# Graph attention layer, last stage: the large piece of scores and flags comes as two pieces, issued behind the landing of the chains' additions

## Chip, cores and metric

One core of one Trainium2 chip runs the whole kernel. The metric is the device time of one execution in microseconds, the median of several runs.

## What is computed

The reference is one layer of a graph network with 6,250 nodes, 200,000 edges (sorted by destination) and 8 heads, with a residual and a layer norm behind it. Cut to what matters here:

```python
qk = jnp.sum(q[:, dst] * rel_k, -1) / 4.0                 # a score for each edge and head
m = segment_max(qk.T, dst); se = segment_sum(exp(qk.T - m[dst]), dst)
lse = log(se) + m                                         # a log-sum for each node and head
logw = qk - lse.T[:, dst]
agg = segment_sum(logw[..., None] * rel_v, dst)           # sums over the edges of a node
z = layer_norm(relu(agg @ z_W + z_b), z_g, z_beta)
x = layer_norm(x + z)
```

As the weights are qk minus lse, the sums over edges fall apart: one sum of qk times rel_v, and one of rel_v alone that is later multiplied by lse. So the edge stage can store sums before any lse is known.

## The kernel before

The first two stages (`start` and `edges`, about 2750 us) compute tables of the nodes and run over the edges in groups of 512. They leave three things in DRAM: `edge_qk`, the scores by head; `edge_fresh`, flags in bf16 that say where a new destination begins; and `tile_sums`, the sums over each tile of 128 edges by destination. A destination whose edges run over several tiles has its sum in parts; the *chains* add these parts along the tiles with a scan, and the results are added onto rows of `tile_sums`.

The last stage (`tail`) has three strands.

- **Log-sums.** 128 partitions (16 chunks of the edges times 8 heads) hold 12,544 scores each in `t_x` and as many flags in `t_fresh`, in 14 sub-pieces of `SUB` = 896 columns (`NSUB` = 14). For each sub-piece k, DVE scans a running maximum (line 1791), computes ratios (1796, 1797, into a ring of `RS` = 4 buffers) and scans the running sum of the sub-piece before (1781). PE subtracts the maximum (2168, 2169), ACT takes the exponential (2016, 2018) and, two sub-pieces later, the logarithm (1998). PE then turns the log-sums of sub-piece k - 3 (2153, 2154), ACT copies them into one of `LR` = 2 buffers `t_lse_sb` (`copy_lse`, 2008 and 2009), and SP stores that buffer, 448 KB, into `edge_lse` (line 1746). `copy_lse(k)` for k of 2 and more waits until store k - 2 has landed. DVE's ratio of sub-piece k waits for PE's turn of sub-piece k - 4.
- **Sums.** POOL first issues 13 indirect DMAs that add the chains' results onto `tile_sums` (line 1694, semaphore `s_add`), waits until all have landed (line 1697), and then gathers the sums of 36 blocks of 128 nodes (line 1703). Then it waits for all stores of log-sums and gathers these by node (line 1711), 49 gathers, with the 13 gathers of sums that are left between them.
- **Turns.** 13 turns of up to four blocks of nodes combine sums and log-sums, multiply with z_W, norm and store; DVE's first row of a turn that needs gathered log-sums is line 1893.

**How scores and flags arrive.** `PARTS` names the pieces in sub-pieces: 0, 1, 2 to 3, 4 to 7, 8 to 13. The first three are loaded in the edge stage. Piece 3 (scores 1792 KB, flags 896 KB) and piece 4 (scores 2688 KB, flags 1344 KB) are loaded in `tail`: the scores by SP, one behind the other, when the chains' last transpose is done (`s_cb` at 7, since the chains use the same columns of `t_x`); the flags by ACT (`load_fresh`), piece 3 early, piece 4 at its sub-piece 1. DVE waits for a piece's semaphore `s_x`, scores and flags, at the piece's first sub-piece. SP's instructions run in order: behind the two issues of scores come the 14 stores of log-sums, then loads of x.

DMAs of SP, of ACT and of POOL go into three queues: in the views q1 is that of SP, q10 that of ACT, q0 that of POOL.

Of the kernel before, what the change touches and what calls it, by code (L numbers as in the profile page):

```python
# [12 lines left out]
KT = -(-E // (P * P))  # L13
# [31 lines left out]
FIRSTS_AT = 385  # L45
NSUB = 14
SUB = CE // NSUB
PARTS = [(0, 1), (1, 2), (2, 4), (4, 8), (8, NSUB)]
HALF = KT * P
CHAIN_AT = GROUPS + 3  # L50
ROWS_AT = GROUPS + 7
# [80 lines left out]
def chain_views(t):  # L132

    x = t["x"]
    st = x[:, PARTS[3][0] * SUB:PARTS[3][0] * SUB + 2 * HALF]
    at = PARTS[3][0] * SUB + 2 * HALF + 32
    return x[:, at:at + 2 * HALF], st, x[:, at + 2 * HALF:at + 3 * HALF]
# [37 lines left out]
class Phase:  # L175
# [8 lines left out]
    def sem(self, name):  # L184
        self.sems.append(self.nc.alloc_semaphore(name=name))
        return self.sems[-1]
# [823 lines left out]
def edges(nc, a, t):  # L1010
# [79 lines left out]
    def is_group(x, loop):  # L1090
# [4 lines left out]
                                                      "chain_back", "chain_back_copied")}  # L1095
    passed.update({f"x_piece{i}": nc.alloc_semaphore(name=f"x_piece{i}") for i in range(len(PARTS))})
    s_fl, s_fm, s_fh, s_more = (passed[n] for n in ("firsts_low", "firsts_mid", "firsts_high", "chains_loaded"))
    s_ct, s_cc, s_cs, s_cb, s_cbc = (passed[n] for n in ("chain_T", "chain_T_copied", "chain_summed", "chain_back", "chain_back_copied"))
    s_x = [passed[f"x_piece{i}"] for i in range(len(PARTS))]

# [12 lines left out]
    with nc.Block(no_gpsimd_drain=True) as block:  # L1113
        @block.sync
        def _(sp):
# [12 lines left out]
            def load_piece(k):  # L1128

                a0, a1 = PARTS[k]  # L1130
                b = -(-((CHUNKS - 1) * CE + a1 * SUB) // BE) - 1
# [444 lines left out]
def tail(nc, a, t, out):  # L1576
# [63 lines left out]
    s_fh, s_ct, s_cc, s_cs, s_cb, s_cbc = (passed[n] for n in ("firsts_high", "chain_T", "chain_T_copied", "chain_summed", "chain_back", "chain_back_copied"))  # L1640
    s_x = [passed[f"x_piece{i}"] for i in range(len(PARTS))]
    s_pre, s_ch, s_add = sem("tail_pads"), sem("tail_dve_chain"), sem("chain_added")
# [16 lines left out]
    def turn(n):  # L1659

        if not 0 <= n < TURNS:
            return None
        whole = n < TURNS - 1 or BLOCKS % NBK == 0 and LAST == P
        return (NBK, P) if whole else (BLOCKS - NBK * n, LAST)
# [18 lines left out]
    with nc.allow_non_contiguous_dma(reason="rows of 512 bytes"), nc.Block(no_gpsimd_drain=True) as block:  # L1683
# [43 lines left out]
        @block.sync  # L1727
        def _(sp):
            rows = t["qk_d"].rearrange("h (c e) -> (h c) e", e=CE)
            sp.wait_ge(s_pre, 1)  # L1730
            sp.dma_start(t["qk_d"][:, E:PLACES], low).then_inc(s_low, 16)
            for k in (3, 4):
                a0, a1_ = PARTS[k]
                sp.wait_ge(s_cb, 7)
                if k == 4:
                    sp.wait_ge(s_low, 16)
                sp.dma_start(x[:, a0 * SUB:a1_ * SUB], rows[:, a0 * SUB:a1_ * SUB]).then_inc(s_x[k], 16)
            def load(n):
                if turn(n):
                    nb, rows = turn(n)  # L1740
                    sp.dma_start(xb[n % XBR][0:rows, 0:nb, :],
                                 a["x"][P * NBK * n:P * NBK * n + nb * rows, :].rearrange("(b p) f -> p b f", p=rows)).then_inc(s_xl[n % XBR], 16)

            for k in range(NSUB):
                sp.wait_ge(s_lc, 2 * (k + 1))
                sp.dma_start(t["lse_d"].rearrange("(e c) h -> e (c h)", c=CHUNKS)[k * SUB:(k + 1) * SUB, :].rearrange("(t p) c -> p t c", p=P), lse_sb[:, k % LR, :, :]).then_inc(s_ls[k % LR], 16)
            sp.wait_ge(s_d, NSUB)
            for n in range(XBR):
                load(n)
            for q in range(LR):  # L1750
                sp.wait_ge(s_ls[q], 16 * len(range(q, NSUB, LR)))
            for n in range(TURNS):
                nb, rows = turn(n)
                sp.wait_ge(s["o"], n + 1)
                sp.dma_start(out[P * NBK * n:P * NBK * n + nb * rows, :].rearrange("(b p) f -> p b f", p=rows), o[n % 2][0:rows, 0:nb, :]).then_inc(s_o[n % 2], 16)
                load(n + XBR)
            for q in range(2):
                sp.wait_ge(s_o[q], 16 * len(range(q, TURNS, 2)))

        @block.vector  # L1760
        def _(dve):
# [22 lines left out]
            for k in range(NSUB):  # L1784
                lo, hi = k * SUB, (k + 1) * SUB
                for part, (a0, _) in enumerate(PARTS):
                    if k == a0:
                        dve.wait_ge(s_x[part], 32)
                if k >= 1:
                    dve.wait_ge(s_m, k)  # L1790
                v.tensor_tensor_scan(out=m[:, lo + 1:hi + 1], data0=fresh[:, lo:hi], data1=x[:, lo:hi],
                                     initial=m[:, lo:lo + 1] if k else -BIG, op0=ALU.add, op1=ALU.max).then_inc(s_m, 1)
                dve.wait_ge(s_m, k + 1)
                if k >= RS:
                    dve.wait_ge(s_t, k - RS + 1)
                link(v.tensor_tensor(out=ratio[:, k % RS, :], in0=m[:, lo:hi], in1=m[:, lo + 1:hi + 1], op=ALU.subtract))
                v.tensor_tensor(out=ratio[:, k % RS, :], in0=ratio[:, k % RS, :], in1=fresh[:, lo:hi], op=ALU.add).then_inc(s_d, 1)
                if k == 0:
                    dve.wait_ge(s_cc, 7)
                    dve.wait_ge(s_cs, 4)  # L1800
                    for half in range(2):
                        chain_scan(v, t, 2, half).then_inc(s_cs, 1)
                if k >= 1:
                    run_sum(k - 1)
# [167 lines left out]
        def _(act):  # L1972
            flags = t["fresh_d"].rearrange("(c e) -> c e", e=CE)

            def load_fresh(k):
                a0, a1_ = PARTS[k]
                act.dma_start(fresh[:, a0 * SUB:a1_ * SUB], flags[:, a0 * SUB:a1_ * SUB].unsqueeze(0).to_broadcast([H, CHUNKS, (a1_ - a0) * SUB])).then_inc(s_x[k], 16)
# [18 lines left out]
            def ln_of(k):  # L1996
                act.wait_ge(s_s, k + 1)
                sc_.activation(ratio[:, k % RS, :], x[:, k * SUB:(k + 1) * SUB], ACT.Ln).then_inc(s_ln, 1)

            def copy_lse(k):  # L2000
                act.wait_ge(s_t, k + 1)
                if k == 0:
                    act.wait_ge(s_low, 16)
                if k >= LR:
                    act.wait_ge(s_ls[k % LR], 16 * (k // LR))
                by_place = lambda ap: ap.rearrange("p t (c h) -> p t c h", h=H)
                by_head = lambda ap: ap.rearrange("p (t h c) -> p t c h", h=H, c=CHUNKS)
                sc_.activation(by_place(lse_sb[:, k % LR, 0:4, :]), by_head(bank[4][:, 0:4 * P]), ACT.Copy).then_inc(s_lc, 1)
                sc_.activation(by_place(lse_sb[:, k % LR, 4:TIL, :]), by_head(bank[5][:, 0:(TIL - 4) * P]), ACT.Copy).then_inc(s_lc, 1)

            for k in range(NSUB):
                lo, hi = k * SUB, (k + 1) * SUB
                if k == 1:
                    load_fresh(4)
                act.wait_ge(s_e, k + 1)
                sc_.activation(x[:, lo:hi].rearrange("p (b e) -> p b e", b=2), banks[:, 2 * (k % 2):2 * (k % 2) + 2, 0:HALF_E], ACT.Exp).then_inc(s_xe, 1)
                act.wait_ge(s_d, k + 1)
                sc_.activation(ratio[:, k % RS, :], ratio[:, k % RS, :], ACT.Exp).then_inc(s_xd, 1)
                if k >= 2:
                    ln_of(k - 2)  # L2020
                if k >= 3:
                    copy_lse(k - 3)
# [228 lines left out]
```

## Time and profile before

| | us |
|---|---|
| median of 3 runs | 3012.12 (3007.8 to 3014.08) |
| the profiled execution | 3012.67 |
| its span, first to last instruction | 3010.8 |
| mean granted TensorE clock, share of full speed | 0.978 |

A row of the timeline gives the start, the length, the engine, the line, the operation with its output and inputs, and in brackets how long the engine was idle ahead of it and what ended that. A row of the waits gives who waited for whom, the total, the count and the longest. A row of the DMA issues gives the size, and behind the last comma the time from issue to landing. "SPq" and "ACTq" rows are issues of DMAs. Over the whole span PE is busy to 93% and DVE to 95%, but these are the edge stage's figures; the last stage begins at about 2755 us.

### The profile page before, as it was taken

The numbers are of one execution on the slowest core, as the hardware profiler recorded it, in microseconds if no ns is written. First come the engines' busy times: TensorE is split into PE (matmuls) and PEld (weight loads), VectorE is DVE, ScalarE is ACT, GpSimd is POOL, SyncE is SP. The second block draws the span as 40 slices with busy tenths as digits, with TensorE's granted clock in tenths as the row PEclk, the third lists the DMA queues.
The fourth block names the chain that finished last, engine by engine and source line by source line (L and its number), as shares of the span: only waits on it lengthen the run. The fifth ranks groups of instructions, "written<-read, shape, count | busy, mean of one in ns | idle before, by whom it ended". The sixth has DMA issues, their size and how long they took to land. (4 is left out here: it accounts for less than half of the span.)

```text
span 3010.8 us, 74627 instructions
## 1 busy us (share of the span) xinstructions
PE 2806.2 (93%) x18674; PEld 2495.0 (83%) x18870; DVE 2848.1 (95%) x3072; ACT 2305.1 (77%) x5301; POOL 2392.3 (79%) x2622
## 2 busy tenths in 40 slices
PE   4659999999999999999999999999999999997945
PEld 3348999999999999999999999999999999995733
DVE  6979999999999999999999999999999999998847
ACT  2548888888888888888888888888888888885536
POOL 5778888888888888888888888888888888885672
PEclk9979999999999999999999999999999999999977
DMA  3568888888888888888888888888888888887542
GB/s 82 160 178 243 258 254 256 255 254 254 254 255 253 257 255 253 254 254 256 254 254 255 254 255 252 256 255 253 256 253 255 252 256 256 252 262 217 153 101 56
DMA packets 660920, 703.01 MB, mean 233 GB/s; under 512 B 98777, under 2 KB 555214, under 8 KB 660469
## 3 DMA queue, kind: packets, MB, share of 16 engines
q1 hardware_dynamic: 568753, 491.48, 54.2%
q0 software_dynamic: 84896, 208.11, 25.1%
q10 hardware_dynamic: 7204, 2.66, 0.5%
q8 instruction: 26, 0.43, 0.1%
q14 instruction: 41, 0.34, 0.0%
HBM read 470.00 MB, written 231.15 MB: 233 GB/s over the span
## 5 line engine op out<-in xcount | busy, mean ns | idle before, releaser
L1446 POOL DMA_INDIRECT e_rows<-node_table,e_gcol x1564 | 1912.3, 1223 | 420.1 <-issue 416.4
L1239 PE MATMUL banks<-w_edge,e_eat 128*128 128x240 f32 x6256 | 1397.0, 366 | 1.0 <-ACT e_ysq L1368 0.7
L1239 PEld LDWEIGHTS banks<-w_edge,e_eat 128*128 128x128 f32 x6256 | 1180.6, 190 | 85.0 <-issue 1.3
L1218 PE MATMUL banks<-e_h,e_oh 128*128 128x248 f32 x3128 | 782.9, 373 | 13.0 <-DVE e_h L1552 2.8
L1547 DVE TENSOR_REDUCE e_zs<-e_z 128x96 f32<-128x1440 f32 x391 | 642.6, 1644 | 0.2
L1218 PEld LDWEIGHTS banks<-e_h,e_oh 128*128 128x128 f32 x3128 | 563.5, 190 | 44.9 <-DVE e_h L1552 4.3
L1331 ACT ACTIVATE e_agg<-banks 128x496 f32<-128x496 f32 x782 | 458.2, 586 | 109.9 <-PE banks L1218 100.1
L1535 DVE TENSOR_TENSOR e_p<-banks,e_yr 128x960 f32<-128x960 f32 x391 | 452.4, 1157 | 27.9 <-PE banks L1239 14.1
L1552 DVE TENSOR_TENSOR e_h<-e_p,e_zw 128x960 f32<-128x960 f32 x391 | 449.5, 1150 | 1.2 <-POOL e_zw L1459 1.2
L1516 DVE TENSOR_TENSOR e_p<-e_p,e_rows 128x960 f32<-128x960 f32 x391 | 449.7, 1150 | 0.0
L1346 ACT ACTIVATE e_eat<-banks 128x512 f32<-128x512 f32 x391 | 233.4, 597 | 282.0 <-PE banks L1252 281.9
L1562 DVE TENSOR_REDUCE e_yvar<-e_ysq 128x64 f32<-128x960 f32 x391 | 448.3, 1147 | 0.0
L1368 ACT ACTIVATE e_ysq<-banks 128x960 f32<-128x960 f32 x391 | 379.9, 972 | 65.0 <-PE banks L1239 27.7
L1354 ACT ACTIVATE e_z<-e_p 128x960 f32<-128x960 f32 x391 | 389.3, 996 | 1.4 <-DVE e_p L1516 1.4
L1290 PE MATMUL banks<-e_q,e_oht 128*128 128x120 bf16 x4692 | 310.2, 216 | 2.1 <-DVE e_z L1525 2.1
L1290 PEld LDWEIGHTS banks<-e_q,e_oht 128*128 128x128 bf16 x4692 | 265.3, 98 | 2.6 <-issue 2.6
L1252 PE MATMUL banks<-ident,e_ea 128*128 128x128 f32 x1564 | 235.9, 274 | 23.2 <-DMA e_ea<-in_edge_attr 22.7
L1525 DVE TENSOR_TENSOR e_z<-e_p,banks 128x480 f32<-128x480 f32 x391 | 253.5, 648 | 0.1
L1252 PEld LDWEIGHTS banks<-ident,e_ea 128*128 128x128 f32 x1564 | 195.1, 141 | 54.7 <-DMA e_ea<-in_edge_attr 24.2
L1403 ACT ACTIVATE e_oht<-banks 128x512 bf16<-128x512 f32 x391 | 231.3, 592 | 0.0
L1382 ACT ACTIVATE e_oh<-banks 128x512 f32<-128x512 f32 x391 | 229.5, 587 | 0.0
L1282 PEld LDWEIGHTS banks<-rank_code,e_feat 128*128 128x128 bf16 x1564 | 120.2, 98 | 45.8
(414 smaller groups left out, 2549.3 us busy)
## 6 DMA issues: line engine op xcount, KB each, us to landing
tile_sums<-e_agg SPq DMA_DIRECT2D x391, 496.0 KB
e_q<-q_by_rank SPq DMA_DIRECT2D x1564, 90.0 KB
e_ea<-in_edge_attr SPq DMA_DIRECT2D x390, 256.0 KB
e_rows<-node_table,e_gcol POOLq DMA_INDIRECT x1564
edge_lse<-t_lse_sb SPq DMA_DIRECT2D x14, 448.0 KB, 3.3
edge_qk<-e_qkt SPq DMA_DIRECT2D x130, 48.0 KB
node_table<-n_tb SPq DMA_DIRECT2D x24, 240.0 KB, 2.9
n_x<-in_x SPq DMA_DIRECT2D x24, 128.0 KB, 2.4
```

Of the source, the lines that this page charges most:

```text
L1218: last = nc.tensor.matmul(sums_bank(x, loop, half)[:, (j % 2) * AW:(j % 2 + 1) * AW], oh[:, x % OR, j, :], hh[:, x % HR, j, :, :].rearrang ...
L1239: last = nc.tensor.matmul(out_ps[:, j // 2, (j % 2) * 2 * HC:(j % 2 + 1) * 2 * HC], eat[:, x % 4, j * P:(j + 1) * P], t["w_edge"][:, at:at ...
L1252: last = nc.tensor.transpose(eat_ps[:, j * P:(j + 1) * P], ea[:, k, j, :], ident[:])
L1290: last = nc.tensor.matmul(qx_ps[:, j * HC:(j + 1) * HC], oht[:, x % 2, j * P:(j + 1) * P], qw[:, k, j, part * HC:(part + 1) * HC], start=( ...
L1331: nc.scalar.activation(agg[:, k, 2 * half:2 * half + 2, :].rearrange("p j c -> p (j c)"), sums_bank(x, loop, half)[:, 0:2 * AW], ACT.Copy) ...
L1354: nc.scalar.activation(z[:, x % ZR, :, 0:2 * H, :], p[:, k, :, :, :, :].rearrange("p t h k c -> p t (h k) c"), ACT.Square).then_inc(s_psq, 1)
L1446: g.indirect_dma_start(out=rows[:, k, j, :], out_offset=None, in_=table, in_offset=bass.IndirectOffsetOnAxis(ap=gcol[:, kb, at:at + 1].bit ...
L1516: v.tensor_tensor(out=p[:, k, :, :, :, :].rearrange("p t h k c -> p (t h k c)"), in0=p[:, k, :, :, :, :].rearrange("p t h k c -> p (t h k ...
L1535: v.tensor_tensor(out=p[:, k, :, :, :, :].rearrange("p (b t) h k c -> p b (t h k) c", b=2), in0=u_ps.rearrange("p b (h c) -> p b h c", c=C ...
L1547: v.tensor_reduce(out=zs[:, x % WR, :, :], in_=z[:, x % ZR, :, :, :], axis=AX.X, op=ALU.add).then_inc(s_z, 1)
L1552: v.tensor_tensor(out=hh[:, x % HR, :, :, 0:2 * C].rearrange("p t h (s c) -> p (t h) s c", s=2), in0=p[:, k, :, :, 1, :].rearrange("p t h ...
L1562: v.tensor_reduce(out=yvar[:, x % 2, :, :], in_=ysq[:, x % 2, :, :].rearrange("p t (h c) -> p t h c", c=C), axis=AX.X, op=ALU.add).then_in ...
```

## The change

The last piece becomes two, sub-pieces 8 to 10 and 11 to 13 (scores 1344 KB, flags 672 KB each). SP waits for the landing of all 13 additions (`s_add` at 16 times 13) ahead of the scores of piece 4; the scores of piece 5 follow behind the wait for `s_low`, the semaphore of a small store of pads. The wait for `s_cb` stands once. ACT issues the flags of piece 4 at its sub-piece 4 and those of piece 5 at its sub-piece 6, where the flags of the one large piece were issued at sub-piece 1. DVE waits for piece 5 at sub-piece 11.

```diff
-PARTS = [(0, 1), (1, 2), (2, 4), (4, 8), (8, NSUB)]
+PARTS = [(0, 1), (1, 2), (2, 4), (4, 8), (8, 11), (11, NSUB)]
@@ sync
-            for k in (3, 4):
+            for k in (3, 4, 5):
                 a0, a1_ = PARTS[k]
-                sp.wait_ge(s_cb, 7)
+                if k == 3:
+                    sp.wait_ge(s_cb, 7)
                 if k == 4:
+                    sp.wait_ge(s_add, 16 * KT)
+                if k == 5:
                     sp.wait_ge(s_low, 16)
                 sp.dma_start(x[:, a0 * SUB:a1_ * SUB], rows[:, a0 * SUB:a1_ * SUB]).then_inc(s_x[k], 16)
@@ scalar
             for k in range(NSUB):
                 lo, hi = k * SUB, (k + 1) * SUB
-                if k == 1:
-                    load_fresh(4)
+                if k in (4, 6):
+                    load_fresh(4 if k == 4 else 5)
                 act.wait_ge(s_e, k + 1)
```

## Rows read from the trace of the kernel before

**Rows 1.** The waits, 2760 to 2880 us: total us, times, longest us.

```profile
POOL t_sums L1703 <- DMA tile_sums<-firsts,carry_idx: 19.5, 1, 19.5
DVE t_ratio L1796 <- PE banks L2154: 6.9, 5, 5.5
PE banks L2153 <- ACT t_lse_sb L2009: 6.5, 4, 3.4
ACT t_lse_sb L2008 <- DMA edge_lse<-t_lse_sb: 6.2, 1, 6.2
DVE t_m L1791 <- DMA t_x<-edge_qk: 0.6, 1, 0.6
```

**Rows 2.** Timeline of DVE, sub-pieces 7 and 8.

```profile
2807.68 2.06 DVE L1791 TENSOR_TENSOR_SCAN t_m<-t_fresh,t_m,t_x 128x896 f32<-128x896 bf16 x1
2815.28 1.09 DVE L1796 TENSOR_TENSOR t_ratio<-t_m 128x896 f32<-128x896 f32 x1 [5.55 <-PE banks L2154]
...
2819.42 2.06 DVE L1791 TENSOR_TENSOR_SCAN t_m<-t_fresh,t_m,t_x 128x896 f32<-128x896 bf16 x1
```

**Rows 3.** Timeline of ACT: copies of log-sums, 0, 2 and 3.

```profile
2790.81 0.49 ACT L2009 ACTIVATE t_lse_sb<-banks 128x384 f32<-128x384 f32 x1
...
2809.10 0.60 ACT L2008 ACTIVATE t_lse_sb<-banks 128x512 f32<-128x512 f32 x1 [6.16 <-DMA edge_lse<-t_lse_sb]
...
2815.22 0.60 ACT L2008 ACTIVATE t_lse_sb<-banks 128x512 f32<-128x512 f32 x1 [2.65 <-PE banks L2154]
```

**Rows 4.** DMA issues: stores issued in 2791 to 2792, 2809 to 2811, 2873 to 2875.

```profile
edge_lse<-t_lse_sb SPq DMA_DIRECT2D x1, 448.0 KB, 17.7
...
edge_lse<-t_lse_sb SPq DMA_DIRECT2D x1, 448.0 KB, 3.0
...
edge_lse<-t_lse_sb SPq DMA_DIRECT2D x1, 448.0 KB, 4.0
```

**Rows 5.** Timeline of POOL: first and last addition, first gathers.

```profile
2762.44 2.76 POOL L1694 DMA_INDIRECT tile_sums<-firsts,carry_idx  x1 [0.19 <-issue]
...
2789.74 2.38 POOL L1694 DMA_INDIRECT tile_sums<-firsts,carry_idx  x1 [0.30 <-issue]
2811.66 1.09 POOL L1703 DMA_INDIRECT t_sums<-tile_sums,sum_idx  x1 [19.53 <-DMA tile_sums<-firsts,carry_idx]
...
2879.05 1.01 POOL L1711 DMA_INDIRECT t_x<-edge_lse,lse_rows  x1 [1.67 <-DMA edge_lse<-t_lse_sb]
```

**Rows 6.** Timeline of DVE, first row of a late turn.

```profile
2934.79 0.19 DVE L1893 TENSOR_TENSOR t_x<-banks,t_x 128x32 f32<-128x32 f32 x1 [4.86 <-DMA t_x<-edge_lse,lse_rows]
```

**Rows 7.** Landing of the 13 additions (line 1694); a gather issued in 2808 to 2812.

```profile
DMA to landing us min/median/max: 7.7/19.7/21.7
...
t_sums<-tile_sums,sum_idx POOLq DMA_INDIRECT x1, 2.8
```

**Rows 8.** POOL's queue: packets, MB, share. 2760-2812, 2762-2780, 2792-2794, 2800-2808, 2811-2816.

```profile
q0 software_dynamic: 1872, 1.65, 23.1%
...
q0 software_dynamic: 483, 0.43, 23.2%
...
q0 software_dynamic: 226, 0.20, 64.8%
...
q0 software_dynamic: 550, 0.49, 38.3%
...
q0 software_dynamic: 96, 0.25, 18.2%
```

**Rows 9.** Stretches: engines' busy us, clock, DMA share and GB/s (last two).

```profile
2744.00:2760.00 16.00, 10.77 (x56) 8.77 (x54) 8.92 (x6) 8.77 (x20) 0.54 (x2) 0.89 0.94 328
2774.00:2800.00 26.00, 19.31 (x90) 12.49 (x89) 24.82 (x17) 11.49 (x15) 15.69 (x9) 1.00 1.04 268
...
2752.00:2754.00 2.00, 0.00 (x0) 0.00 (x0) 0.00 (x0) 0.29 (x2) 0.00 (x0) 1.00 0.96 373
```

**Rows 10.** Timeline of SP: the issues of the scores of pieces 3 and 4.

```profile
2771.47 1.17 SPq L1737 DMA_DIRECT2D t_x<-edge_qk  x2
```

## Prediction, made before the changed kernel ran

> **What bounds the kernel now.** The change touches only the last 250 us of a span of 3010.8 us, so I read that stage alone. First the chain of waits between 2760 and 2880 us [rows 1]: the reader is to see one long wait of POOL for the chains' additions, and three waits that are one stall handed on. ACT waits 6.2 us for a store of log-sums, PE waits for ACT's copy, DVE waits 5.5 us for PE. Then the timeline of DVE [rows 2] and of ACT [rows 3]: DVE runs its 14 pieces nearly back to back and loses time at one place, in piece 7, where the row before ends at 2809.74 and the next starts at 2815.28. ACT was ready for its third copy at 2809.10 - 6.16 = 2802.94; the copy needs the buffer that store 0 (lines 1744 to 1746) empties. Store 0 was issued between 2791 and 2792, as the first copy ended at 2791.30, and landed 17.7 us later [rows 3, 4], where the third one needed 3.0: it stood behind the 2688 KB of the large piece, issued on the same queue at about 2772.
>
> Next, who sets the end. POOL's first gather of log-sums starts at 2879.05, released by the last store, 1.67 us after POOL was free [rows 5]. From there on DVE's turns wait for those gathers, as late as 2934.79 [rows 6], and what follows is DVE's own work. So the end hangs on the chain "store 0, ACT, PE, DVE, last store, gathers", and 1.67 us behind it on POOL's 36 gathers of sums, which began only at 2811.66, when the last addition had landed [rows 5].
>
> **The change, part by part.** *Additions land sooner.* In the kernel before, the first addition, which has only flags beside it, lands in 7.7 us; the median, beside the large pieces, is 19.7 us [rows 7]. All 13 additions take 1872 packets up to 2812 us, 144 each; 483 were through by 2780 [rows 8]. With only the 1792 KB piece issued at 2771.5 (8 rows of 14 KB for each of 16 DMA engines, some 7 us at the rates of [rows 9]), the rings hold nothing but additions from about 2780. I estimate 560 packets done by then, as the flags of the last six pieces no longer compete. In a stretch with few other packets 226 went in 2 us, 113 per us [rows 8]; POOL issues 13 additions in 2792.1 - 2762.4 = 29.7 us [rows 5], 144 packets in 2.3 us or 63 per us. The seven issued by 2780 leave 450 packets waiting, cleared in 450/(113 - 63) = 9 us, so before POOL's last issue, which ends at 2789.74 + 2.38 = 2792.12 [rows 5]. That last one meets the flags of piece 4, which ACT now issues behind its copy at 2791.3 [rows 3], 672 KB; the first addition met flags too, and landed at 2762.44 + 7.7 = 2770.1, 4.9 us behind the end of its issue at 2765.2 [rows 5, 7]. So the additions are all in at T = 2792.12 + 4.9 = 2797.0. Low end: a gather lands 2.8 - 1.1 = 1.7 us behind the end of its issue [rows 5, 7], which gives 2793.8. High end in the rivals.
>
> *POOL's gathers* start at T and not at 2811.66, 14.7 us sooner, and so end about 14 us sooner. Alone that is worth at most the 1.67 us, as the last store ends later than POOL.
>
> *The pieces move behind a wait on SP.* What is queued behind them on SP are the stores of log-sums; store 0 was issued before T and is now held until T and then stands behind both pieces. This is the term that decides. From T on the rings carry 2688 KB = 2.75 MB of scores, then store 0, 0.46 MB, and beside them POOL's gathers, 0.25 MB in 5 us [rows 8], so some 0.6 MB: 3.8 MB. Rates: 268 GB/s beside additions and flags, 328 GB/s with SP's queue alone [rows 9], hence 14.2 or 11.6 us; I take the middle, 12.9, since the new stretch lies between the two. Fixed parts: 0.7 us for two issues (1.17 us was the pair's stretch before, [rows 10]; I count the issue of each at some 0.36) and 1.4 us, what a store of 3.0 us holds beyond its 0.46 MB at those rates. Store 0 lands at 2797.0 + 0.7 + 1.4 + 12.9 = 2812.0, against 2809.1 before: **+2.9 us** (ends: 2793.8 + 13.7 = 2807.5, -1.6; 2800.5 + 16.3 = 2816.8, +7.7). ACT, PE and DVE follow it as before: 6.2 us from the copy to DVE's row at 2815.28. DVE has no slack afterwards, so it passes to the last store undiminished.
>
> *Piece 3 alone on SP's queue* saves DVE the 0.6 us wait [rows 1], but that lies ahead of the stall and is swallowed by it: 0.
>
> *Pieces 4 and 5 in time?* DVE reads piece 4 in its row at 2819.42 [rows 2], now about 2822, and piece 5 three pieces later. Piece 4 lands at about T + 9 = 2806, its flags before. Piece 5's flags are issued by ACT after the third copy, at about 2813. No wait: 0. Cover gone only if T passed 2812.
>
> *ACT's two issues of flags*, below 1 us each if they cost what a piece's issue costs SP [rows 10], fall into ACT's waits for PE (2.65 us in the piece behind the stalled copy [rows 3]): 0. One more wait, one more semaphore and one more DMA on SP: 0.
>
> *The last store* took 4.0 us beside POOL's gathers, the undisturbed one 3.0 [rows 4]; POOL is through by about 2863, so I count **-0.8 us** (bounds -1.0 and 0).
>
> Sum: +2.9 - 0.8 = +2.1 us. The profiled execution took 3012.67 us (span 3010.8) and would take 3014.8; against the median of the runs, 3012.12, it is **3014.2 us**. The stall is not removed: its cause was a store behind a large piece, and it stands behind the same bytes again, issued later but against emptier rings.
>
> The Trainium skill, "DMA: Bandwidth & Descriptors", Specifications, gives a core's share of HBM as about 358 GB/s; by it the 3.8 MB would need 10.6 us, an estimate, and store 0 would land about 2 us sooner than I have it. The trace agrees for short stretches only: its best two microseconds here show 373 GB/s, its long ones 268 and 328 [rows 9].
>
> **The rivals.** *Fast transfer* (no change): with the additions gone the pieces run at the best rate seen, 373 GB/s: 10.2 us, store 0 at 2797.0 + 2.1 + 10.2 = 2809.3, the stall as before, end -0.6 us, 3011.5. For it: 2752 to 2754 us. Against it: it held for 2 us, with stores in it. The page named above speaks for a rate near this one.
>
> *Slow additions* (slower): the additions drain at the rate of 2800 to 2808 us, where 550 packets went in 8 us, 69 per us [rows 8], though the rings were busy to 0.6 only. Then 1872 - 560 = 1312 packets need 19 us from 2780: T = 2799, and with the flags and the landing about 2800.5. Store 0 at 2816.8, +7.7 - 0.8 = +6.9: 3019.0 to 3019.6. It decides once T lies past 2800. For it: that stretch itself. Against it: 113 per us in 2792 to 2794, and that the slow stretch had small store packets in turn with the additions.
>
> *Additions no sooner* (the change doesn't do what it says): if their 20 us were their own and not the neighbours', T stays near 2811, store 0 at 2826, +16 us, 3028. Against it: the first landed in 7.7 us.
>
> *The store passes the pieces* (faster): if its packets don't stand behind the pieces', it lands 3.3 us after T + 0.7, 2801, before ACT asks at 2802.94. The stall of 5.5 us goes and the 0.6 us and 0.8 us become real: -6.9 us, 3005.2. Against it: the 17.7 us of store 0 before [rows 4].
>
> **How the numbers follow.** Forecast (store 0 between 2807.5 and 2815) 0.55, fast transfer 0.17, slow additions 0.17, additions no sooner 0.03, passing store 0.08. The bound of 0.2% is 6 us, about what a measurement of this kernel can tell from no change (its three runs lie 6.3 us apart). Slower: 0.17 + 0.03 = 0.20. Faster: 0.08. Same: 0.72. The range leaves out the passing store and the late additions (0.11 together), with some 2 us for the scatter of the runs on both ends: 3009.7 - 2.2 and 3019.0 + 1.5, so 3007.5 to 3020.5.
>
> **What would show it.** Right: POOL's first gather of sums near 2797; SP's pieces issued then and store 0 behind them; ACT still idle 6 to 10 us for store 0 ahead of its third copy; DVE still idle in piece 7; POOL idle some 18 us ahead of its first gather of log-sums, and that gather near 2881. Wrong: no wait of ACT for a store (passing store), the first gather of sums past 2800 (slow additions), or DVE waiting for scores in piece 8.

## The result, and the profile after

The changed kernel takes 3016.06 us (median of 20 runs) where the kernel before takes 3010.83 us: a ratio of 1.0018, 95% interval 1.0012 to 1.0024. Two of the 20 runs of the kernel before took 3783.1 and 4595.6 us; the ratio is that of the fast runs and leaves them out. In a second series it was 1.0021 (1.0011 to 1.0030). So the change costs some 5 to 6 us, clear of the scatter once so many runs are taken; whether it lies under or over the 0.2% that stood as the bound of "no change" can't be told, as both intervals hold that bound. The time lies inside the stated range; the forecast was +2.1 us.

The profiled execution after took 3020.54 us, its span is 3018.8 us. Its last stage began later than that of the kernel before, which is the edge stage's scatter, so all times of the stage are counted from **S**, the start of DVE's first row of the stage (line 1773 before, 1776 after): 2761.65 before, 2763.54 after. From S to the end of the span it is 249.2 us before and 255.3 us after.

First the waits of the kernel after in 2760 to 2885 us, to be held against [rows 1]:

```profile
POOL t_x L1711 <- DMA edge_lse<-t_lse_sb: 11.6, 1, 11.6
...
DVE t_ratio L1799 <- PE banks L2157: 10.5, 6, 8.8
...
ACT t_lse_sb L2011 <- DMA edge_lse<-t_lse_sb: 8.3, 1, 8.3
...
POOL t_sums L1703 <- DMA tile_sums<-firsts,carry_idx: 8.2, 1, 8.2
```

POOL's wait for the additions fell from 19.5 to 8.2 us: the change does what it says. But ACT's wait for store 0 rose from 6.2 to 8.3 us and DVE's from 5.5 to 8.8 us, and POOL now idles 11.6 us for the last store. Then the timelines of DVE, ACT, POOL and SP in the kernel after, for [rows 2, 3, 5, 10]:

```profile
2763.54 0.06 DVE L1776 MEMSET t_m<- 128x1 f32 x1 [3.57 <-PEq L1113]
...
2821.29 1.09 DVE L1799 TENSOR_TENSOR t_ratio<-t_m 128x896 f32<-128x896 f32 x1 [8.85 <-PE banks L2157]
```

```profile
2793.44 0.61 ACTq L1980 DMA_DIRECT2D t_fresh<-edge_fresh  x1
...
2813.99 0.60 ACT L2011 ACTIVATE t_lse_sb<-banks 128x512 f32<-128x512 f32 x1 [8.34 <-DMA edge_lse<-t_lse_sb]
```

```profile
2792.86 1.68 POOL L1694 DMA_INDIRECT tile_sums<-firsts,carry_idx  x1 [0.30 <-issue]
2802.72 2.13 POOL L1703 DMA_INDIRECT t_sums<-tile_sums,sum_idx  x1 [8.18 <-DMA tile_sums<-firsts,carry_idx]
...
2884.44 1.01 POOL L1711 DMA_INDIRECT t_x<-edge_lse,lse_rows  x1 [11.59 <-DMA edge_lse<-t_lse_sb]
```

```profile
2801.80 0.81 SPq L1740 DMA_DIRECT2D t_x<-edge_qk  x2
...
2802.66 77.97 SPq L1749 DMA_DIRECT2D edge_lse<-t_lse_sb  x14
```

The reader is to see the order: ACT issues the flags of piece 4 at 2793.44, inside the issue of the last addition. That addition lands only some 7 us behind the end of its issue at 2794.54; SP, which waits for it, issues the scores of pieces 4 and 5 from 2801.80 on and store 0 at 2802.66; ACT gets its buffer at 2813.99.

### The profile page after: what moved, and what is told of

It is laid out like the page before. It is cut to its first block and busy times, and to the rows that moved or that the text cites. A ratio compares the mean times of both kernels' runs of the same rounds, so it can differ in the third digit from the quotient of the medians.

```text
span 3018.8 us, 74825 instructions
## 1 busy us (share of the span) xinstructions
PE 2828.1 (94%) x18870; PEld 2500.0 (83%) x18870; DVE 2848.2 (94%) x3072; ACT 2307.4 (76%) x5301; POOL 2399.0 (79%) x2622
```

## The experiments

In the diffs "-" is the kernel named as the base. Two columns carry the readings: S to the end of the span, and S to POOL's first gather of log-sums; the difference is the stretch of the turns. DVE's wait is that in sub-piece 7.

| kernel | ratio to before (95%) | ACT waits for store 0 | DVE waits | S to gather | S to end |
|---|---|---|---|---|---|
| before, three profiles | 1.000 (0.9991 to 1.0009) | 6.2, 5.2, 4.5 | 5.6, 4.6, 2.3 | 117.4, 116.0, 114.9 | 249.2, 249.1, 247.3 |
| after, three profiles | 1.0018, 1.0021 | 8.3, 8.3, 7.8 | 8.9, 8.9, 8.5 | 120.9, 121.0, 122.3 | 255.3, 255.3, 256.2 |
| split_only | 0.9997 (0.9988 to 1.0006) | 2.0 | 0.3 | 111.7 | 245.6 |
| flags_early | 0.9993 (0.9984 to 1.0002) | 3.0 | 0.8 | 111.7 | 246.1 |
| flags_late_only | 0.9999 (0.9990 to 1.0008) | none | 0.3 | 111.5 | 246.6 |
| flags_at_5 | 1.0021 (1.0010 to 1.0032) | 7.3 | 6.7 | 120.7 | 253.2 |
| wait_only | 1.0042 (1.0028 to 1.0056) | 14.7 | 15.1 | 126.3 | 261.0 |
| stores_first | 0.9993 (0.9984 to 1.0002) | none | 0.3 | 114.1 | 245.9 |
| stores_and_flags | 0.9991 (0.9982 to 1.0000) | none | 0.3 | 111.2 | 246.0 |
| short_rows | 1.0000 (0.9991 to 1.0009) | 3.8 | 1.6 | 113.0 | 242.6 |

**before_again** and **before_third** are the kernel before, **after_again** and **after_third** the changed one, with no edit.

> The kernel before, unchanged, for a second profile. Theory A (the last turns scatter from run to run): the stretch from POOL's first gather of log-sums to the end of the span, 131.8 us in the profile before and 134.4 us in the one after, comes out anywhere between 131 and 135 us, and the stage's start (DVE's first row of the stage, 2761.7 before, 2763.5 after) scatters by a few us too. Rival B (the longer turns belong to the change): it comes out at 131.8 within 0.3 us. Ratio to before 1.000 within 0.0006.

> The changed kernel, unchanged, beside the others of this call. Theory A (the stall and its size belong to the kernel, the turns to the run): the last addition again lands 8 to 9 us behind its issue, ACT waits 8 us for store 0, DVE 8 to 9 us in piece 7; from DVE's first row of the stage to POOL's first gather of log-sums 120 to 121 us (120.9 in the first profile; 117.4 and 116.0 in the two profiles of the kernel before); ratio to before 1.0012 to 1.0024. Rival B (the first profile was an odd one): the stall is near 5 us, that stretch near 117, ratio 1.000 to 1.001.

> One look, for a third profile of the kernel before. From DVE's first row of the stage to the end of the span 249.1 us in the first two, of which 131.8 and 133.1 us from POOL's first gather of log-sums on. Theory A (the stretch of the turns belongs to the run): 131 to 135 us. Rival B (it belongs to the kernel): 131.5 to 133.2 us.

> One look, for a third profile of the changed kernel. From DVE's first row of the stage to the end of the span 255.3 us in the first two, of which 134.4 and 134.3 us from POOL's first gather of log-sums on. Theory A (the stretch of the turns belongs to the run): 131 to 135 us. Rival B (it belongs to the kernel): 134.2 to 134.5 us.

The stall belongs to the kernels: 8.5 to 8.9 us in all profiles of after, 2.3 to 5.6 us in those of before, of which mine had the longest. The turns took 131.8, 133.1 and 132.4 us before and 134.4, 134.3 and 133.9 us after. The wide range of theory A, 131 to 135 us, holds all of them, and rival B is out (133.1 is more than 0.3 us from 131.8, and 133.9 lies outside 134.2 to 134.5); yet the two kernels don't overlap, and three profiles of each are too few to tell that from chance. The stretch with the stall, S to POOL's first gather, has means of 116.1 us before and 121.4 us after: these 5.3 us are about what the runs show. The third profile of after reached its stall on another way:

```profile
2790.76 1.09 DVE L1799 TENSOR_TENSOR t_ratio<-t_m 128x896 f32<-128x896 f32 x1 [3.27 <-PE banks L2157]
...
2818.24 1.09 DVE L1799 TENSOR_TENSOR t_ratio<-t_m 128x896 f32<-128x896 f32 x1 [8.54 <-PE banks L2157]
```

```profile
2791.86 1.09 POOL L1703 DMA_INDIRECT t_sums<-tile_sums,sum_idx  x1 [3.01 <-DMA tile_sums<-firsts,carry_idx]
```

DVE lost 3.3 us earlier, so ACT came to its sub-piece 4 later and issued the flags only at 2790.70, when the additions were almost in (POOL waited 3.0 us and not 8.2). The flags then ran beside the scores, and store 0 was as late as ever: ACT still waited 7.8 us.

**split_only** undoes the wait and the move of the flags, and keeps the two pieces (base: the changed kernel).

```diff
-                if k == 3:
-                    sp.wait_ge(s_cb, 7)
-                if k == 4:
-                    sp.wait_ge(s_add, 16 * KT)
-                if k == 5:
+                sp.wait_ge(s_cb, 7)
+                if k == 4:
                     sp.wait_ge(s_low, 16)
...
-                if k in (4, 6):
-                    load_fresh(4 if k == 4 else 5)
+                if k == 1:
+                    load_fresh(4)
+                    load_fresh(5)
```

> The changed kernel without the wait for the additions: pieces 4 and 5 are two DMAs, scores issued right behind piece 3, both flags at sub-piece 1, as the one large piece was before. Theory A (what costs is where the bytes stand, not how many DMAs carry them): additions land in about 20 us as before, POOL's first gather of sums about 50 us behind the stage's start, ACT waits 6 to 7 us for store 0, DVE 5 to 6 us in piece 7; ratio to before 1.000 (0.9993 to 1.0007). Rival B (one more piece, semaphore and DMA cost in themselves): 1.001 to 1.002, like the whole change.

The ratio is as expected, the mechanism is not: I had expected the stall of the kernel before, and it is gone. Timelines of ACT and of POOL in split_only:

```profile
2801.75 0.60 ACT L2008 ACTIVATE t_lse_sb<-banks 128x512 f32<-128x512 f32 x1 [1.99 <-DMA edge_lse<-t_lse_sb]
```

```profile
2803.36 2.12 POOL L1703 DMA_INDIRECT t_sums<-tile_sums,sum_idx  x1 [14.72 <-DMA tile_sums<-firsts,carry_idx]
```

So two pieces of scores and of flags, with the same bytes at the same time, are better for store 0 than one. From S to POOL's first gather the wait and the late flags cost some 10 us (121.4 against 111.7), more than the whole change does; the ratio, with its interval, doesn't show that.

**flags_early** leaves the wait and issues the flags of piece 4 at sub-piece 1.

```diff
-                if k in (4, 6):
-                    load_fresh(4 if k == 4 else 5)
+                if k in (1, 6):
+                    load_fresh(4 if k == 1 else 5)
```

> The changed kernel with the flags of piece 4 issued at sub-piece 1 and not at sub-piece 4; all else as changed. Theory A (in the changed kernel the last addition needed 8.9 us because it met these flags, others 4.2): the last addition lands 4 to 5 us sooner behind POOL's last issue, SP issues the pieces and store 0 that much sooner, DVE's wait in piece 7 falls from 8.9 to about 4.5 us; ratio to before 1.0002 to 1.0006. Rival B (the additions need their time by themselves): landing 8 to 9 us, DVE's wait 8 to 9 us, ratio 1.0018.

Timelines of POOL and ACT in flags_early:

```profile
2792.13 1.09 POOL L1703 DMA_INDIRECT t_sums<-tile_sums,sum_idx  x1 [3.13 <-DMA tile_sums<-firsts,carry_idx]
```

```profile
2803.19 0.60 ACT L2011 ACTIVATE t_lse_sb<-banks 128x512 f32<-128x512 f32 x1 [3.04 <-DMA edge_lse<-t_lse_sb]
```

POOL's wait for the last addition is 3.1 us where it was 8.2, and with these 5 us ACT's wait falls from 8.3 to 3.0 us and DVE's from 8.9 to 0.8 us: the whole loss and the old stall with it. Theory A stands; the gain is larger than I had put it (1.0002 to 1.0006). DVE gained some 3 us more than ACT: from ACT's copy to DVE's row it took 4.6 us here and 7.3 us in the changed kernel, and PE's granted clock in that stretch was 1.00 of full speed here, the upper level, and 0.54 there (next section).

```profile
2803.70:2808.00 4.30, 3.75 (x31) 3.53 (x31) 3.46 (x3) 3.24 (x6) 3.75 (x2) 1.00 0.91 239
```

**flags_late_only** is split_only with the flags at sub-pieces 4 and 6: the move of the flags without the wait (base: split_only).

```diff
-                if k == 1:
-                    load_fresh(4)
-                    load_fresh(5)
+                if k in (4, 6):
+                    load_fresh(4 if k == 4 else 5)
```

> As split_only, with the flags issued as in the changed kernel, at sub-pieces 4 and 6: the move of the flags alone, without the wait. Theory A (late flags hurt because SP holds store 0 until the additions that they delay have landed; without that wait store 0 is issued at once and the scores are long through): additions land no later than in split_only, no wait of DVE above 2 us, ratio 0.9985 to 1.0005. Rival B (late flags hurt by themselves, as bytes ahead of store 0): ACT waits 5 us or more for store 0, ratio 1.0007 or more.

No stall at all; ACT's third copy follows PE, not a store:

```profile
2801.06 0.60 ACT L2008 ACTIVATE t_lse_sb<-banks 128x512 f32<-128x512 f32 x1 [0.53 <-PE banks L2154]
```

So four kernels with two pieces make a square: neither the wait alone (flags_early, 0.9993) nor the late flags alone (0.9999) costs anything that the runs show against split_only (0.9997), both together give 1.0018 to 1.0021. The wait holds SP, and store 0 with it; the late flags lengthen what is waited for.

**flags_at_5** moves the flags of piece 4 behind the additions. In its profile ACT issued them at 2797.58, 3.7 us behind SP's issue of store 0 at 2793.87.

```diff
-                if k in (4, 6):
-                    load_fresh(4 if k == 4 else 5)
+                if k in (5, 6):
+                    load_fresh(4 if k == 5 else 5)
```

> The changed kernel with the flags of piece 4 issued at sub-piece 5, behind the landing of the additions, and not at sub-piece 4; all else as changed. Theory A (the flags hurt because they meet the last addition): the last addition lands about 4 us behind its issue, DVE's wait in piece 7 is 1 to 4 us (the flags now run beside the pieces ahead of store 0), ratio 0.9993 to 1.0005. Rival B (flags must be early, out of the way of everything): the loss only moves, DVE's wait stays 7 us or more, ratio 1.0012 or more.

Timelines of POOL and ACT in flags_at_5:

```profile
2793.92 2.70 POOL L1703 DMA_INDIRECT t_sums<-tile_sums,sum_idx  x1 [4.46 <-DMA tile_sums<-firsts,carry_idx]
```

```profile
2810.92 0.60 ACT L2011 ACTIVATE t_lse_sb<-banks 128x512 f32<-128x512 f32 x1 [7.26 <-DMA edge_lse<-t_lse_sb]
```

My theory fell here: the additions land in time, and the loss is the same. From the issue of store 0 to ACT's copy it is 2810.92 - 2793.87 = 17.1 us, against 2803.19 - 2792.07 = 11.1 us in flags_early. So the meeting with the last addition isn't the only way to lose. The flags ran neither beside the additions nor ahead of store 0 here, but beside it: behind the scores, in 2802.5 to 2808.7, SP's queue q1 moved 995 packets of some 0.5 KB, those of stores 0 and 1, while ACT's queue q10 moved 107 rows of flags. In flags_early, with no flags beside them, it moved 1198 such packets in 2 us, 2801.2 to 2803.2. First flags_at_5, then flags_early:

```profile
q10 hardware_dynamic: 107, 0.58, 38.6%
q1 hardware_dynamic: 995, 0.50, 29.5%
```

```profile
q1 hardware_dynamic: 1198, 0.60, 100.1%
```

In the third profile of after the flags ran beside the scores. So where SP holds store 0 until the additions have landed and sends the scores ahead of it, 672 KB of flags anywhere between the last addition and the landing of store 0 cost about the same; what they run beside differs.

**wait_only** undoes the split: one piece of scores behind the wait, its flags at sub-piece 4.

```diff
-PARTS = [(0, 1), (1, 2), (2, 4), (4, 8), (8, 11), (11, NSUB)]
+PARTS = [(0, 1), (1, 2), (2, 4), (4, 8), (8, NSUB)]
...
-            for k in (3, 4, 5):
+            for k in (3, 4):
...
-                if k == 5:
...
-                if k in (4, 6):
-                    load_fresh(4 if k == 4 else 5)
+                if k == 4:
+                    load_fresh(4)
```

> The changed kernel without the split: one piece of scores (2688 KB) behind the landing of the additions, its flags (1344 KB) at sub-piece 4. Theory A (the flags meet the last addition, packets against packets, so flags twice as long hurt more): the last addition lands 10 to 13 us behind its issue, ACT waits 10 to 14 us for store 0, ratio 1.002 to 1.0035. Rival B (only the bytes ahead of store 0 count, and these are as many as in the changed kernel): ACT waits 8 us, ratio 1.0018.

Twice the flags, 1344 KB, in the same place: POOL waits 14.3 us for the additions, ACT 14.7 us for store 0, and the kernel is 12.3 us slower than before, more than theory A had it (1.002 to 1.0035). The split, which halves these flags, saves half of what the wait and the late flags cost.

```profile
2815.59 0.60 ACT L2010 ACTIVATE t_lse_sb<-banks 128x512 f32<-128x512 f32 x1 [14.71 <-DMA edge_lse<-t_lse_sb]
```

**stores_first** lets store 0 go ahead of the wait, and the scores of piece 5 behind store 2; the flags stay late. **stores_and_flags** is that with the flags of piece 4 at sub-piece 1 as in flags_early.

```diff
-            for k in (3, 4, 5):
...
+            sp.wait_ge(s_cb, 7)
+            scores(3)
...
             for k in range(NSUB):
                 sp.wait_ge(s_lc, 2 * (k + 1))
                 sp.dma_start(t["lse_d"]...then_inc(s_ls[k % LR], 16)
+                if k == 0:
+                    sp.wait_ge(s_add, 16 * KT)
+                    sp.wait_ge(s_low, 16)
+                    scores(4)
+                if k == 2:
+                    scores(5)
```

> The changed kernel with another order on SP: store 0, then the wait for the additions and the scores of piece 4, stores 1 and 2, then the scores of piece 5. Theory A (the stall is store 0 standing behind the wait and the pieces): ACT's wait for store 0 is gone, DVE's wait in piece 7 below 1 us, the last store 8 to 9 us sooner than in the changed kernel, and all of it reaches the end; ratio to before 0.9975 to 0.9985. Rival B (the loss lies in the turns, or POOL or the loads of x take over the end): the wait goes but the time stays within 2 us of the changed kernel's, ratio 1.001 to 1.002.

> Both cures at once: flags of piece 4 at sub-piece 1, and SP's order of store 0, piece 4, stores 1 and 2, piece 5. Theory A (the two cures take away the same stall): no wait of DVE for store 0, last addition landed 3 to 4 us behind its issue, 110.5 to 112 us from DVE's first row of the stage to POOL's first gather of log-sums, ratio 0.998 to 0.9993, the same as each cure alone within 0.0005. Rival B (two separate losses): 0.9975 or less.

The stall for store 0 is gone in both, at late and at early flags, and both cures together are no better than each alone: it is one loss. The gain of stores_first was too high in my expectation, by 2.4 us or more (0.9985 was its least): 3.3 us came back as a wait of DVE for PE in sub-piece 4. In stores_and_flags, which lies in its range, the turns took 134.8 us, 3.0 us more than in the first profile before.

```profile
2789.87 1.09 DVE L1801 TENSOR_TENSOR t_ratio<-t_m 128x896 f32<-128x896 f32 x1 [3.26 <-PE banks L2159]
```

**short_rows** is split_only with the scores of pieces 4 and 5 as three DMAs each (base: split_only).

```diff
-                sp.dma_start(x[:, a0 * SUB:a1_ * SUB], rows[:, a0 * SUB:a1_ * SUB]).then_inc(s_x[k], 16)
+                for b in ([(a0, a1_)] if k == 3 else [(j, j + 1) for j in range(a0, a1_)]):
+                    sp.dma_start(x[:, b[0] * SUB:b[1] * SUB], rows[:, b[0] * SUB:b[1] * SUB]).then_inc(s_x[k], 16)
...
-                        dve.wait_ge(s_x[part], 32)
+                        dve.wait_ge(s_x[part], 64 if part >= 4 else 32)
```

> As split_only (no wait for the additions, both flags at sub-piece 1), with the scores of pieces 4 and 5 as three DMAs each, rows of 3.6 KB where split_only has 10.8 KB and the kernel before 21.5 KB. Theory A (the queues take turns row by row, so shorter rows let the additions and the stores through): median landing of the additions 8 to 12 us (15.1 in split_only, 19 to 19.7 before), the last one 8 us or more sooner than in split_only, no wait of DVE for store 0; ratio 0.9985 to 0.9997. Rival B (only the bytes on the rings count): landing 14 to 16 us as in split_only, POOL's first gather of sums as late.

A miss: the ratio is 1.0000, the median landing is 13.6 us and the last addition lands no sooner (POOL waits 15.1 us). The short stretch from S to the end, 242.6 us, is no gain in the stall: the turns took 129.6 us in this one profile. Queue q0, packets in 8 us from S + 18 on, in the kernel before, in split_only, in short_rows and in flags_late_only:

```profile
q0 software_dynamic: 85, 0.08, 6.4%
```

```profile
q0 software_dynamic: 180, 0.15, 12.5%
```

```profile
q0 software_dynamic: 388, 0.34, 27.4%
```

```profile
q0 software_dynamic: 549, 0.48, 38.7%
```

Halving the rows doubles what gets through beside the scores, and cutting them to a third doubles it once more, as if the queues took turns by rows. But the length of the rows isn't all: flags_late_only has the rows of scores of split_only and no flags beside them in these 8 us, and 549 packets went. In short_rows the scores lose what the additions gain (SP's queue moved 1.33 MB in these 8 us, 1.79 MB in split_only), and the landing of the additions stays.

Why store 0 is better off in split_only than before isn't settled by this, but the traces show what it lands with. In the kernels without the wait and with early flags ACT's third copy starts just ahead of POOL's first gather of sums: by 1.9 to 2.6 us in the three profiles before, 1.6 us in split_only, 0.2 us in short_rows. In the kernel before, SP's queue moved 1052 packets of some 0.5 KB in the 8 us from 2803.7 on, so stores and no row of scores, beside 355 packets of additions:

```profile
q1 hardware_dynamic: 1052, 0.53, 25.7%
...
q0 software_dynamic: 355, 0.31, 24.5%
```

There the last 5 us of store 0's way, up to 2809, were spent beside the additions and not behind the scores. No run tested this alone.

## Why the prediction was right, and where its steps were not

The direction and the range came out (slower by less than the bound or by just more, which the intervals leave open), and the chain store 0, ACT, PE, DVE, last store, gathers is the one that the profile shows. Of the signs on record ACT's wait of 8.3 us, store 0 behind the pieces and DVE's idle time in piece 7 came. One sign against it came too: the first gather of sums is at 2802.72, or 2800.83 counted from the S of the kernel before, past 2800. And POOL idled 11.6 us ahead of the gathers of log-sums, not some 18: its 36 gathers took 70.1 us where they took 65.7 before, which costs nothing while it idles. The sum was 3 to 4 us short, and inside it two terms were off and met.

*The landing of the additions* was mis-sized. Forecast T = 2797.0, 35.3 us behind S; SP issued the scores at 2801.80, 38.3 us behind S, so T was some 2.9 us late. The rate was right in kind: alone on the rings, in 2782 to 2790, 668 packets went in 8 us, 84 per us (113 forecast), with the rings busy to 0.65, so nothing was left over. Wrong was the price of the flags: the last addition landed 8.9 us behind the start of its issue, 7.2 us behind its end, where 4.9 stood in the sum. POOL woke 0.9 us later still, which SP didn't wait for. Landing of the 13 additions in the kernel after, and q0 in 2782 to 2790:

```profile
DMA to landing us min/median/max: 3.8/6.3/8.9
```

```profile
q0 software_dynamic: 668, 0.59, 64.7%
```

*The transfer* was mis-sized the other way. From SP's issue to ACT's copy it is 2813.99 - 2801.80 = 12.2 us where the sum had 15.0. The rings moved 368 GB/s, not the middle of 268 and 328: the rival "fast transfer" was right in this, and with its 10.2 us the sum has 12.3. The figure that the Trainium skill, "DMA: Bandwidth & Descriptors", Specifications, gives for HBM (358 GB/s) was nearer than that middle, and the measured rate lies above it. In the kernel after (span of the stretch, engines, clock, DMA share, GB/s):

```profile
2804.00:2813.00 9.00, 5.25 (x28) 3.39 (x26) 8.08 (x5) 1.65 (x2) 7.78 (x5) 1.00 1.00 368
```

Together they put store 0 at S + 50.45, forecast 2812.0 - 2761.65 = S + 50.35. That agreement is chance: 2.9 us too short in one term, 2.8 us too long in the other.

*"ACT, PE and DVE follow it as before"* was 1.1 us short: from the copy to DVE's row it is 7.3 us after, 6.2 before. PE works in this stretch after one in which it stood idle (in 2810 to 2814 after, in 2807 to 2809.7 before), and its granted clock is 0.54 of full speed after and 0.70 before, 0.50 being the lower level, 1.2 GHz:

```profile
2814.50:2821.30 6.80, 6.19 (x29) 6.13 (x30) 0.01 (x1) 3.03 (x6) 5.16 (x6) 0.54 0.92 214
```

```profile
2809.70:2815.30 5.60, 5.08 (x29) 5.01 (x30) 0.05 (x2) 2.94 (x5) 3.04 (x3) 0.70 0.46 130
```

*The last store* gave back 0.6 us, 0.8 forecast: DVE's row of sub-piece 7 is 4.1 us later against S, the gathers 3.5 us.

*What the old stall was* is half right in the prediction: store 0 stood behind the large piece until about 2803, and the rest of its way, some 5 us, it went beside the additions (see short_rows). The sum has no term for that.

*The size of the old stall* came from one profile, the one with the longest: 5.6 us, where the other two have 4.6 and 2.3 us. Against their mean of 4.2 us the stall grew by 4.6 us and not by 3.3.

*The turns*, which the sum moved as they are, took 2.6 us more. Middle of the turns, before and after:

```profile
2939.10:2979.10 40.00, 27.31 (x80) 16.90 (x79) 33.12 (x82) 26.87 (x82) 19.35 (x18) 0.78 0.21 50
```

```profile
2944.40:2984.40 40.00, 28.21 (x76) 18.12 (x75) 32.53 (x78) 24.80 (x75) 19.55 (x19) 0.71 0.21 50
```

The granted clock is 0.71 against 0.78. Over all 14 profiles, in the same 40 us of the turns, 0.71 goes with turns of 133.9 to 134.7 us, 0.76 to 0.78 with 131.8 to 133.1, and 0.88 (short_rows) with 129.6; but flags_late_only and stores_and_flags, at 0.80 there and at 0.60 in the last part, took 135.0 and 134.8. The means of three profiles, 132.4 before and 134.2 after, lie 1.8 us apart. What sets the clock of a run in the turns stays open: flags_early has the low one without a stall, flags_at_5 the high one with a stall of 6.7 us.

*Weighed rivals.* "Slow additions" gave the right T and a difference, +6.9 us, nearer to the measured 5 to 6 than the forecast's +2.1, for the wrong reason. Its rate of 69 packets per us did not come; the flags did it, and its slow transfer didn't come either. "Additions no sooner" and "the store passes the pieces" fell: POOL's wait fell by 11 us, and store 0 landed behind the scores. I had seen that the late flags meet the last addition, and had not asked what the change would be without late flags; flags_early answers that, and the loss is gone.

As for a version that beats both: flags_early and stores_and_flags, at 3007.25 and 3007.36 us, are 2.7 to 2.8 us below the kernel before of their series; their intervals, which reach 1.0002 and 1.0000, lie under those of the changed kernel, so they beat that one; that they beat the kernel before isn't shown.

## What to carry to other kernels

A wait put ahead of a DMA holds everything behind it on that queue: look up what else the queue must issue, and let short transfers that someone waits for go first. Bytes moved out of the way of one transfer stand in the way of the next, so ask for each stretch of a saturated ring which transfer is waited for, and move only what nobody needs there. Short packets that someone waits for are held up by long rows that are issued behind them, too. A size that rests on one profile of a stall should be read from several: this one varied between 2.3 and 5.6 us.

## What the runs showed of the hardware

An indirect addition of 128 rows of 992 bytes lands in 3.8 to 4.2 us when it has the rings to itself, in about 20 us beside rows of 14 to 21.5 KB, and in 8.9 us beside flags in rows of 5.4 KB. 672 KB of flags cost the transfer beside them about as much whether it was the additions (8.2 against 3.1 us of waiting) or the packets of stores (17.1 against 11.1 us): these packets of 0.5 KB went at 599 per us alone and at 160 per us beside the flags' rows. With scores and a store on SP's queue and POOL's gathers beside them the rings moved 368 GB/s over 9 us, where the best 9 us of the kernel before around its last stage, 2750.5 to 2759.5, have 351 GB/s.
